# Value rounds of four batches of the 64-wide attention made while experts choose their tokens, and the first batch's first rounds at the expert stage's end

## The chip, the cores and the metric

One NeuronCore of a Trainium2 chip runs the whole kernel. The metric is the device time of one execution in microseconds (us); lower is better. PE is TensorE, DVE VectorE, ACT ScalarE, POOL GpSimd, SP the SyncE queue that issues most DMAs.

## The reference

Eight batches of 256 tokens, 256 wide, go through seven stages in float32. The change touches the second and the third: a mixture of experts where each expert chooses its tokens, and a cross-attention of 16 heads that are 64 wide.

```python
x = x + _L0_xattn_ref(_layernorm(x), ctx, ctx, ...)              # stage a0
x = x + _L0_ffn_ref(_layernorm(x), router_w1, router_w2, w1, w2, w3)   # stage f1
    probs = softmax((silu(h @ router_w1) @ router_w2).transpose(0, 2, 1))
    weights, tokens = top_k(probs, 64)               # 16 experts, 64 tokens each
    out = (silu(rows @ w1) * (rows @ w2)) @ w3       # then scatter-add by token
x = x + _L1_xattn_ref(_layernorm(x), ctx, ctx, Wq, bq, Wk, bk, Wv, bv, Wo)   # stage a2
    Q = h @ Wq.T + bq;  K = ctx @ Wk.T + bk;  V = ctx @ Wv.T    # 256 -> 1024
    out = softmax(Q K.T / 8) V, then @ Wo.T
```

K and V of stage a2 depend on the context and on weights alone, not on x.

## The kernel before

Every product is made of float32r halves: a value is split into a high part (ACT rounds it) and a low part (DVE subtracts), and each product is three passes. PE, DVE, ACT, POOL and SP each run their own program and meet by semaphores; a block barrier stands between stages.

**Stage f1** (`expert_choice_ffn`). PE transposes the normalised rows, makes the router's hidden layer and the logits. DVE then chooses 64 of 256 by eight rounds of max, max_index and match_replace (`choose`), PE turns the result over (`transpose_slots`), POOL gathers the first experts' rows from DRAM, and PE transposes them (`transpose_rows`). While `choose` and the gathers run PE has no work. Then come 16 experts: `up` and `down` on PE, about 18 us each, with gates on ACT, products on DVE and the scatter-add into x in DRAM (`scatter`) on POOL. SP writes the rows at the start (h_rows, x_rows), loads each next expert's weights, fetches the attention's weights (`prefetch`), and at the end reads x back as the scatters land. After its last scaling DVE makes the low parts of the attention's weights (`heads_low`), and the block ends.

**Stage a2** (`head_attention`). A batch has 16 steps s (head pair c = s // 2, half of the queries). In a step PE makes the scores of step s, transposes the probabilities of step s - 3, in every second step multiplies a pair's probabilities by the values (`weighted_values`, c = 0 to 7 at steps 5, 7, ... 15, and 1 and 3 of the next batch), and makes one projection round of the next batch. `output(b - 1)` stands at step 5; it waits for the low part of the pair c = 7, which DVE makes in step 4. The rounds are placed by a hand-written table; numbers from 16 on are steps of the batch's own run:

```python
STEP = {"hT": 6, ("k", 0): 7, ("q", 0): 8, ("k", 1): 10, ("q", 1): 11, ("v", 0): 12, ("k", 2): 13, ("v", 1): 14, ("q", 2): 15,
        ("k", 3): NU + 1, ("q", 3): NU + 2, ("v", 2): NU + LAG, ("v", 3): NU + LAG + 1}
```

A k or q round is 12 matmuls of 256 columns. ACT and DVE read it one step later into `k_fresh` or `q_fresh`, and SP copies it by six (k) or four (q) DMAs of 128 KB into the layout of the scores (`place`); ACT waits for that copy before it overwrites the buffer with the next k or q round. A v round is 6 matmuls of 512 columns, and DVE copies it into `vb`. The first batch has no earlier one to hide its rounds in: it makes `early` (k0, hT, v0, q0, v1, k1) before its first scores, and the others by `FIRST_STEP` in its steps 0 to 4. Batches 1 to 6 are a hardware loop on PE, DVE and ACT.

## Time and profile before

| | us |
|---|---|
| median of 3 runs | 1634.62 (1627.76 to 1641.94) |
| the profiled execution | 1631.33 |
| its span, first to last instruction | 1629.5 |
| PE busy | 1404.8 (86%) |
| DVE busy | 1078.6 (66%) |
| ACT busy | 841.1 (52%) |
| POOL busy | 480.4 (29%) |

Times within the trace are counted from the span's start. Stage f1 lasts from about 231 us to 576 us, stage a2 from there to about 997 us; a batch in the middle of a2 takes 49.0 us. A row of the timeline has start, duration, engine, line, operation with output<-input, and in brackets the idle time before it and what ended it. Durations of neighbours on one engine overlap, since operations are pipelined: the pitch is start to start.

### The profile page before, as it was taken

To read this page: it belongs to the slowest core of one execution; us is meant where nothing else is said; L and a number is where in the kernel's file an instruction comes from. 1 tells how busy PE (TensorE), PEld (TensorE's weight loads), DVE (VectorE), ACT (ScalarE), POOL (GpSimd) and SP (SyncE) were. 2 spreads that over 40 slices of the span, in tenths; PEclk is the share of its full clock that TensorE was granted. 3 is DMA by queue.
4 is the path that set the end of the run, shared out by engine and by line. 5 is a ranking of instruction groups with operands and counts; after the bars stand their busy time and mean duration, and the time that the engine had idled before them with its cause. 6 is when DMAs were issued, how large, how long until landed. Compare 5 with 4: busy or idle time off the path is not lost. (4 is left out here: it accounts for less than half of the span.)

```text
span 1629.5 us, 29259 instructions
## 1 busy us (share of the span) xinstructions
PE 1404.8 (86%) x9650; PEld 1133.9 (70%) x9650; DVE 1078.6 (66%) x2481; ACT 841.1 (52%) x1960; POOL 480.4 (29%) x426
## 2 busy tenths in 40 slices
PE   4899883999999959999999996599957799888885
PEld 4666552888888747888888884499945688655553
DVE  4577654666666557777877777644457774588776
ACT  2466652444444436666766676155534453565451
POOL 2111002577777530000000001255422521133343
PEclk7699996999999969999999999599978999899897
DMA  4322134456555456545544454022264010221110
GB/s 145 122 84 89 61 104 168 125 151 154 139 132 142 77 140 147 120 115 129 137 115 115 99 161 138 23 78 76 69 210 136 21 40 19 85 80 63 64 48 26
DMA packets 140110, 168.92 MB, mean 104 GB/s; under 512 B 20136, under 2 KB 131880, under 8 KB 137448
## 3 DMA queue, kind: packets, MB, share of 16 engines
q1 hardware_dynamic: 115032, 131.43, 27.9%
...
q14 instruction: 44, 0.36, 0.1%
...
## 5 line engine op out<-in xcount | busy, mean ns | idle before, releaser
L1046 DVE TENSOR_REDUCE a_nmax<-a_s 128x2 f32<-128x512 f32 x256 | 170.6, 684 | 99.6 <-PE a_s L961 99.1
L1245 ACT ACTIVATE a_probT<-a_t 128x512 f32<-128x512 f32 x256 | 151.8, 601 | 158.3 <-PE a_t L965 129.3
L63 POOL TENSOR_TENSOR a_rstd<-a_veps,minus_half 128x2 f32<-128x2 f32 x24 | 17.2, 715 | 413.8 <-DVE a_veps L57 413.7
L597 ACT ACTIVATE a_prob<-a_score,a_nmax 128x256 f32<-128x256 f32 x256 | 120.0, 479 | 35.0 <-DVE a_nmax L490 34.7
L490 DVE TENSOR_REDUCE a_nmax<-a_score 128x2 f32<-128x512 f32 x128 | 87.7, 685 | 73.5 <-PE a_score L383 73.4
L1782 POOL DMA_INDIRECT x_rows<-early_hn,scatter_row x60 | 129.5, 2158 | 16.4 <-issue 16.4
L1726 ACT ACTIVATE f_gate<-f_gate 128x512 f32<-128x512 f32 x64 | 38.3, 599 | 128.9 <-PE f_gate L1531 110.6
L1641 DVE TENSOR_TENSOR f_y<-f_gate,f_value 128x512 f32<-128x512 f32 x64 | 44.0, 687 | 82.0 <-PE f_value L1531 82.0
L606 ACT COPY a_probT<-a_T 128x512 f32<-128x512 f32 x128 | 76.1, 595 | 22.2 <-PE a_T L391 21.1
L497 DVE TENSOR_SCALAR a_prob<-a_prob,a_rinv 128x256 f32<-128x256 f32 x256 | 83.1, 367 | 4.6
L1542 PE MATMUL f_z<-area_odd_parts,f_y_hi 128*128 128x256 f32 x384 | 84.8, 287 | 0.4
L391 PE MATMUL a_T<-ident,a_prob 128*128 128x128 f32 x512 | 77.0, 273 | 4.2 <-DVE a_prob L497 4.2
L961 PE MATMUL a_s<-area_odd_parts 48*128 48x256 f32 x256 | 59.1, 330 | 24.8 <-DVE a_nmax L1046 14.9
L961 PE MATMUL a_s<-a_ka,a_qa 48*128 48x256 f32 x256 | 62.1, 348 | 17.9 <-DMA a_qa<-a_m_lo 6.2
L961 PEld LDWEIGHTS a_s<-area_odd_parts 48*128 48x128 f32 x256 | 37.0, 192 | 54.7 <-issue 29.1
L1531 PE MATMUL f_gate<-f_rowsT_hi,area_odd_parts 128*128 128x512 f32 x192 | 71.7, 400 | 1.5 <-DVE f_rowsT_lo L1629 1.5
L961 PEld LDWEIGHTS a_s<-a_ka,a_qa 48*128 48x128 f32 x256 | 40.0, 207 | 47.0 <-issue 30.9
L981 PE MATMUL a_o<-a_probT,a_vb 128*32 128x256 f32 x1024 | 71.7, 399 | 1.1 <-ACT a_probT L1245 1.1
L382 PE MATMUL a_score<-a_k_hi,a_q 128*128 128x256 f32 x256 | 70.3, 297 | 2.7 <-DMA a_q<-a_q_fresh_lo 2.0
L1531 PE MATMUL f_value<-f_rowsT_hi,area_odd_parts 128*128 128x512 f32 x192 | 71.3, 399 | 0.0
L402 PE MATMUL a_o<-a_probT,a_vb 128*64 128x256 f32 x512 | 69.4, 392 | 1.2 <-ACT a_probT L606 1.2
...
## 6 DMA issues: line engine op xcount, KB each, us to landing
...
a_k_hi<-a_k_fresh_hi SPq DMA_DIRECT2D x128, 128.0 KB, 2.4
...
a_k_lo<-a_k_fresh_lo SPq DMA_DIRECT2D x64, 128.0 KB, 2.4
a_q<-a_q_fresh_lo SPq DMA_DIRECT2D x64, 128.0 KB, 2.4
a_q<-a_q_fresh_hi SPq DMA_DIRECT2D x62, 128.0 KB, 2.4
a_ctxT<-in_ctxT SPq DMA_DIRECT2D x48, 128.0 KB, 2.7
...
```

Source lines behind the costliest of these rows:

```text
L391: last = nc.tensor.transpose(ps_T[u % 2][:, kc, i, :], prob[:, u % NPROB, i, kc * P:(kc + 1) * P], chip.ident[:, :])
L490: nc.vector.tensor_reduce(nmax[:, u % NPROB, :], ps_score[u % NB][:, :, :], AX.X, ALU.max, negate=True).then_inc(sem["nmax"], 1)
L497: last = nc.vector.tensor_scalar(prob[:, u % NPROB, i, :], prob[:, u % NPROB, i, :], rinv[:, u % NPROB, i:i + 1], None, ALU.mult)
L597: last = nc.scalar.activation(prob[:, u % NPROB, i, :], ps_score[u % NB][:, i, :], ACT.Exp, bias=nmax[:, u % NPROB, i:i + 1], accum_out=rs ...
L606: nc.scalar.copy(probT[:, c % 2, :, :, qt * P:(qt + 1) * P], ps_T[u % 2][:, :, :, :]).then_inc(sem["probT"], 1)
L961: last_s = nc.tensor.matmul(ps_s[i][:, half, :], qa[rows, u % RING, j, half * P:(half + 1) * P], ka[rows, u % RING, j, :], start=True, sto ...
L981: last = nc.tensor.matmul(ps_o[r * STRIP:(r + 1) * STRIP, :], vb[:, f % NV, kc, 4 * g + r, :], probT[:, (PPG * n + r // 2) % NPT, r % 2, k ...
L1046: nc.vector.tensor_reduce(nmax[:, u % 2, :, i * PPU + j], ps_s[i][:, :, :], AX.X, ALU.max, negate=True).then_inc(sem["nmax"], 1)
L1245: nc.scalar.activation(probT[:, t % NPT, i, :, :], ps_t[i][:, :, :], ACT.Exp).then_inc(sem["exp"], 1)
L1531: last = nc.tensor.matmul(ps[f % 2][:, :], W[:, kc, f * P:(f + 1) * P], h[:, kc, :], start=(kc == 0 and i == 0), stop=(kc == KC - 1 and i ...
L1542: last = nc.tensor.matmul(ps_z[s // 2][:, s % 2, :], h[:, f, s * P:(s + 1) * P], W[:, f, :], start=(f == 0 and i == 0), stop=(f == NF - 1 ...
L1782: nc.gpsimd.indirect_dma_start(chip.x_rows, bass.IndirectOffsetOnAxis(ap=scatter_row[:, q, s:s + 1], axis=0), chip.z_last[:, s, :] if last ...
```

## The change

A new `wide_front` holds what both stages share: the context of a batch, six PSUM banks, semaphores, and a DRAM tensor for values.

In stage f1, SP first loads four contexts (batches 1 to 4, eight DMAs of 128 KB) and the weights Wv are loaded a stage earlier. POOL rounds Wv and the contexts, DVE subtracts. After the logits PE makes 16 value rounds (4 batches x 4): ten ahead of `transpose_slots`, six behind it. ACT copies each into one of eight SBUF slots, SP writes each (256 KB) to DRAM. The low parts of Wk, Wq move from the end of the stage into the last expert's products, in pieces of 1024 columns; the first batch's context is loaded and split there, and after the last `down` PE makes k0, v0, v1, k1, v2, v3 of batch 0.

In stage a2, batch 0 begins with hT and q0; ACT instead of DVE copies its four v rounds; q3 moves from step 3 to step 4. Batches 1 to 4 have no v rounds: SP fetches each half of `vb` by one DMA of 512 KB, the first at step 12 of the batch before, ahead of the placing of q1, the second at step 4. Batches 5 to 7 are as before. The loops over batches are written out.

On PE, in stage f1, the order before had nothing between the last logits and the two turning operations (f_z<-f_routerT is the logits, f_slots the chosen tokens, early_hn the first gathered rows):

```order
L1496 MATMUL f_gate<-f_hT,area_odd 128x512 x2
L1504 MATMUL f_z<-f_routerT,area_odd 128x256 x4
L1511 MATMUL f_T<-ident,f_slots 128x128 x2
L1520 MATMUL f_T<-ident,early_hn 128x128 x8
L1531 MATMUL f_gate<-f_rowsT_hi,area_odd_parts 128x512
```

Now the last value round of sixteen, and the five before it of which one is shown, stand between the slots and the gathered rows (f_y_hi and f_y_lo hold the contexts here):

```order
L1654 MATMUL a2f_bank<-f_Wv_hi,f_y_hi 128x512 x2
L1654 MATMUL a2f_bank<-area_even_parts,f_y_hi 128x512 x2
L1654 MATMUL a2f_bank<-f_Wv_hi,f_y_lo 128x512 x2
L1654 MATMUL f_z<-f_Wv_hi,f_y_hi 128x512 x2
L1654 MATMUL f_z<-area_even_parts,f_y_hi 128x512 x2
L1654 MATMUL f_z<-f_Wv_hi,f_y_lo 128x512 x2
L1589 MATMUL a2f_bank<-ident,early_hn 128x128 x8
```

Ten more such rounds stand ahead of the slots. On PE, in steps 3 to 5 of a batch of a2, before (a_o is `weighted_values` of c = 7, 128x512 are v2 and v3; the product with a_oT_hi, the output, follows):

```order
L402 MATMUL a_o<-a_probT,a_vb 64x256 x4
L334 REGISTER_ALU
L362 MATMUL a_proj<-area_odd_parts,a_ctx_hi 128x512 x2
L362 MATMUL a_proj<-area_even_parts,a_ctx_hi 128x512 x2
L362 MATMUL a_proj<-area_odd_parts,a_ctx_lo 128x512 x2
L38 REGISTER_ALU
L382 MATMUL a_score<-a_k_hi,a_q 128x256
L383 MATMUL a_score<-a_k_lo,a_q 128x256
L382 MATMUL a_score<-a_k_hi,a_q 128x256
L383 MATMUL a_score<-a_k_lo,a_q 128x256
L391 MATMUL a_T<-ident,a_prob 128x128 x4
```

and in a batch without v rounds now:

```order
L447 MATMUL a2f_bank<-a_probT,a_vb 64x256 x4
L421 MATMUL a2f_bank<-a_k_hi,a_q 128x256
L422 MATMUL a2f_bank<-a_k_lo,a_q 128x256
L421 MATMUL a2f_bank<-a_k_hi,a_q 128x256
L422 MATMUL a2f_bank<-a_k_lo,a_q 128x256
L430 MATMUL a2f_bank<-ident,a_prob 128x128 x4
L421 MATMUL a2f_bank<-a_k_hi,a_q 128x256
L422 MATMUL a2f_bank<-a_k_lo,a_q 128x256
L421 MATMUL a2f_bank<-a_k_hi,a_q 128x256
L422 MATMUL a2f_bank<-a_k_lo,a_q 128x256
L430 MATMUL a2f_bank<-ident,a_prob 128x128 x4
L462 MATMUL a_proj<-area_odd_parts,a_oT_hi 128x256
```

The steps 3 and 4 have only scores, transposes and the one product with the values ahead of the output. On SP, at step 12, the fetch of values now stands between the placing of k1 and of q1:

```order
L329 DMA a_k_hi<-a_k_fresh_hi 64x2x256 x2
L329 DMA a_k_lo<-a_k_fresh_lo 64x2x256
L336 DMA a_vb<-a2f_values 128x2x512
L329 DMA a_q<-a_q_fresh_hi 64x2x256
L329 DMA a_q<-a_q_fresh_lo 64x2x256
```

Before, the copies of q1 followed those of k1 directly. The diff, cut to its core:

```diff
+    p.v_slots = 8
...
+    p.staged = range(1, 5)
+    p.v_dram = nc.dram_tensor(f"{stage}_values", (len(p.staged) * P, TB * 4 * D), F32).ap()
+    p.rounds = [("k", 0), ("v", 0), ("v", 1), ("k", 1), ("v", 2), ("v", 3)]
...
-    early = [("k", 0), "hT", ("v", 0), ("q", 0), ("v", 1), ("k", 1)]
-    FIRST_STEP = {("q", 1): 0, ("k", 2): 1, ("q", 2): 2, ("k", 3): 3, ("q", 3): 3, ("v", 2): 4, ("v", 3): 4}
+    early = ["hT", ("q", 0)]
+    FIRST_STEP = {("q", 1): 0, ("k", 2): 1, ("q", 2): 2, ("k", 3): 3, ("q", 3): 4}
...
+    VALUES_STEP = LAG + NCH + 1
...
+    without_v = [name for name in rounds if name[0] != "v"]
+    SPLIT_V = [f for f in range(B) if f not in p.staged]
...
+    def order(f):
+
+        return first_rounds if f == 0 else without_v if f in p.staged else rounds
...
         else:
-            own = [name for name in rounds if STEP[name] + delay == NU + s]
-        return [(name, b) for name in own] + [(name, b + 1) for name in rounds if more and STEP[name] + delay == s]
+            own = [name for name in order(b) if STEP[name] + delay == NU + s]
+        return [(name, b) for name in own] + [(name, b + 1) for name in (order(b + 1) if more else ()) if STEP[name] + delay == s]
...
+            if first(f) and name in ahead:
+                return ahead[name]
...
-            context(0)
...
+            def fetch_values(f, half):
+
+                sp.wait_ge(sem["pv"], (f - 1) * NCH + (half + 1) * NCH // 2)
+                values = p.v_dram[p.staged.index(f) * P:(p.staged.index(f) + 1) * P, :].rearrange("p (j e) -> p j e", j=TB)
+                at = slice(half * BANK, (half + 1) * BANK)
+                sp.dma_start(vb[:, :, at], values[:, :, at]).then_inc(sem["v_back"], 16)
+
             def places(b, more, part=None):
                 for s in range(NU):
+                    if s == VALUES_STEP and b + 1 in p.staged:
+                        fetch_values(b + 1, 0)
+                    if s == LAG + 1 and b in p.staged:
+                        fetch_values(b, 1)
...
+            for i in range(p.v_slots):
+                sp.wait_ge(p.sem[f"v_stored{i}"], 16 * (NV * len(p.staged) // p.v_slots))
...
                 if c % (NCH // 2) == 0:
-                    pe.wait_ge(sem["vb"], b * NV + (1 if c == 0 else 2) * TB)
+                    halves = 1 if c == 0 else 2
+                    if b in p.staged:
+                        pe.wait_ge(sem["v_back"], 16 * (2 * p.staged.index(b) + halves))
+                    else:
+                        pe.wait_ge(sem["vb"], SPLIT_V.index(b) * NV + halves * TB)
+                if first(b) and c == 1:
+                    pe.wait_ge(*consumed(0, ("k", 1)))
...
-            with pe.Fori(1, B - 1) as b:
-                batch(b, True)
-            batch(B - 1, False)
+            pe.wait_ge(sem["vb"], NV)
+            pe.wait_ge(*consumed(0, ("k", 0)))
+            for b in range(B):
+                batch(b, b + 1 < B)
...
-            context_low(0)
+            read_round(0, ("k", 0))
...
+            read_round(0, ("k", 0))
             zeros(0)
-            for name in early:
-                read_round(0, name)
-                if name == "hT":
-                    zeros(1)
-                if name == ("q", 0):
-                    place_first_queries()
-            batch(0, True)
-            with act.Fori(1, B - 1) as b:
-                batch(b, True)
-            batch(B - 1, False)
+            keep_first_v(0)
+            read_round(0, "hT")
+            for i in range(1, NV):
+                keep_first_v(i)
+            read_round(0, ("q", 0))
+            place_first_queries()
+            zeros(1)
+            read_round(0, ("k", 1))
+            for b in range(B):
+                batch(b, b + 1 < B)
...
+        V_SLOTS, V_BANKS, V_BEFORE = p.v_slots, 4, 10
+        values = [(f, half, t) for f in p.staged for half in range(2) for t in range(TB)]
+        staging = hT[:, :, :].rearrange("p k t -> p (k t)")
+        ps_T, ps_gate, ps_value = p.banks[0:2], p.banks[2:4], p.banks[4:6]
...
+            for n, f in enumerate(p.staged):
+                for kc in range(KC):
+                    sp.dma_start(raw_context[n][:, kc, :], chip.ctxT_dram[kc * P:(kc + 1) * P, f * S:(f + 1) * S]).then_inc(sem["v_context"], 16)
...
+            for n, (f, half, t) in enumerate(values):
+                sp.wait_ge(sem["v_kept"], n + 1)
+                rows_of_batch = slice(p.staged.index(f) * P, (p.staged.index(f) + 1) * P)
+                at = t * 4 * D + half * BANK
+                slot = n % V_SLOTS
+                sp.dma_start(p.v_dram[rows_of_batch, at:at + BANK], staging[:, slot * BANK:(slot + 1) * BANK]).then_inc(p.sem[f"v_stored{slot}"], 16)
...
+            for kc in range(KC):
+                sp.dma_start(p.ctxT[:, kc, :], chip.ctxT_dram[kc * P:(kc + 1) * P, 0:S]).then_inc(p.sem["ctx"], 16)
...
+            def value_round(n):
+
+                f, half, t = values[n]
+                h = p.staged.index(f)
+                if n == 0:
+                    pe.wait_ge(sem["v_lo"], KC)
+                pe.wait_ge(sem["v_context_lo"], h + 1)
+                if n >= V_BANKS:
+                    pe.wait_ge(sem["v_kept"], n - V_BANKS + 1)
+                _, _, Wv_lo = heads["v"]
+                hi, lo = context_hi[h], context_lo[h]
+                passes = [(c, W, kc) for c, W in ((hi, Wv_hi), (hi, Wv_lo), (lo, Wv_hi)) for kc in range(KC)]
+                for i, (c, W, kc) in enumerate(passes):
+                    last = nc.tensor.matmul(v_banks[n % V_BANKS][:, :], c[:, kc, t * P:(t + 1) * P], W[:, kc, half * BANK:(half + 1) * BANK],
+                                            start=(i == 0), stop=(i == len(passes) - 1))
+                last.then_inc(sem["v_ready"], 1)
+
+            for n in range(V_BEFORE):
+                value_round(n)
             transpose_slots()
+            for n in range(V_BEFORE, len(values)):
+                value_round(n)
             pe.wait_ge(sem["slot"], 4)
+            pe.wait_ge(sem["v_kept"], len(values))
             transpose_rows(0, 0, 0)
             pair_of(0, True)
...
+            def round_ahead(name, ps):
+
+                what, i = name
+                W, W_hi, W_lo = heads[what]
+                if what == "k":
+                    pe.wait_ge(sem["heads_lo"], KC)
+                else:
+                    W_hi = Wv_hi
+                if what == "v":
+                    half, j = divmod(i, TB)
+                    passes = [(c, W, kc) for c, W in ((p.ctx_hi, W_hi), (p.ctx_hi, W_lo), (p.ctx_lo, W_hi)) for kc in range(KC)]
+                    for n, (c, W, kc) in enumerate(passes):
+                        last = nc.tensor.matmul(ps[:, :], c[:, kc, j * P:(j + 1) * P], W[:, kc, half * BANK:(half + 1) * BANK],
+                                                start=(n == 0), stop=(n == len(passes) - 1))
+                else:
+                    passes = [(W, c, kc) for W, c in ((W_hi, p.ctx_hi), (W_hi, p.ctx_lo), (W_lo, p.ctx_hi)) for kc in range(KC)]
+                    for o in range(2):
+                        c0 = (2 * i + o) * P
+                        for n, (W, c, kc) in enumerate(passes):
...
+            pe.wait_ge(p.sem["ctx_lo"], 1)
+            for name, ps in zip(p.rounds, ahead):
+                round_ahead(name, ps)
...
+                        if last_expert:
+                            heads_low(f - 1)
...
+                    if last_expert:
+                        context_low()
+                        heads_low(3)
+                    weigh(e, q, last_expert)
...
-                    heads_low()
-                    dve.wait_ge(sem["heads_lo"], 1)
+                    nc.vector.tensor_scalar(heads["bq"], heads["bq"], heads["scale"], None, ALU.mult).then_inc(sem["heads_lo"], 1)
+                    dve.wait_ge(sem["heads_lo"], 2 * KC + 1)
...
+            _, _, Wv_lo = heads["v"]
+            for kc in range(KC):
+                dve.wait_ge(sem["v_hi"], kc + 1)
+                nc.vector.tensor_tensor(Wv_lo[:, kc, :], heads["v"][0][:, kc, :], Wv_hi[:, kc, :].bitcast(F32), ALU.subtract).then_inc(sem["v_lo"], 1)
+            low_weights(0, 0, 0)
+            for n in range(len(p.staged)):
+                dve.wait_ge(sem["v_context_hi"], n + 1)
+                nc.vector.tensor_tensor(context_lo[n], raw_context[n], context_hi[n].bitcast(F32), ALU.subtract).then_inc(sem["v_context_lo"], 1)
+            for n in range(1, 3):
...
-                        heads_high()
+                        context_high()
+                        heads_high(4)
+                        heads_high(5)
...
+            for n in range(len(values)):
+                act.wait_ge(sem["v_ready"], n + 1)
+                slot = n % V_SLOTS
+                if n >= V_SLOTS:
+                    act.wait_ge(p.sem[f"v_stored{slot}"], 16 * (n // V_SLOTS))
+                nc.scalar.copy(staging[:, slot * BANK:(slot + 1) * BANK], v_banks[n % V_BANKS][:, :]).then_inc(sem["v_kept"], 1)
...
+            for kc in range(KC):
+                nc.gpsimd.tensor_copy(Wv_hi[:, kc, :], heads["v"][0][:, kc, :]).then_inc(sem["v_hi"], 1)
             for g in range(E_G, GROUPS):
                 norm_rstd(nc, pool, chip, sem, nb, GT, g - E_G, g * GT)
+            pool.wait_ge(sem["v_context"], 16 * KC * len(p.staged))
+            pool.wait_ge(sem["hn"], GROUPS - E_G)
+            for n in range(len(p.staged)):
+                nc.gpsimd.tensor_copy(context_hi[n], raw_context[n]).then_inc(sem["v_context_hi"], 1)
...
+    w.values = (w.WvT, rows("WvT"))
...
-        dmas = [(w.WqT, rows("WqT")), (w.WkT, rows("WkT")), (w.WvT, rows("WvT")), (w.bq, a[prefix + "bq"]), (w.bk, a[prefix + "bk"])]
+        dmas = [(w.WqT, rows("WqT")), (w.WkT, rows("WkT")), *([w.values] if narrow else []), (w.bq, a[prefix + "bq"]), (w.bk, a[prefix + "bk"])]
```

## Rows read from the trace of the kernel before

**Rows 1.** Windows: length, busy time of PE, PEld, DVE, ACT, POOL, PEclk, DMA share, GB/s.

```profile
246.00:274.00 28.00, 2.89 (x12) 1.97 (x11) 15.41 (x56) 2.97 (x6) 8.34 (x11) 0.59 0.64 233
676.00:725.00 49.00, 47.87 (x368) 40.80 (x364) 36.92 (x103) 34.03 (x108) 0.69 (x1) 1.00 0.52 124
```

**Rows 2.** Timeline of PE, from the end of the experts to the first scores.

```profile
567.02 0.28 PE L1542 MATMUL f_z<-f_W_hi,f_y_lo 128*128 128x256 f32 x1
582.52 0.80 PE L370 MATMUL a_proj<-a_ctx_hi,area_odd_parts 128*128 128x256 f32 x2 [15.22 <-DVE a_ctx_lo L456]
...
592.14 0.40 PE L370 MATMUL a_proj<-a_hT_hi,area_even_parts 128*128 128x256 f32 x2
...
598.04 0.36 PE L382 MATMUL a_score<-a_k_hi,a_q 128*128 128x256 f32 x1 [1.97 <-DMA a_q<-a_q_fresh_lo]
```

**Rows 3.** Timeline of SP at the start of a2: x comes back.

```profile
577.51 3.29 SPq L291 DMA_DIRECT2D x_tok<-x_rows  x2
```

**Rows 4.** Timeline of DVE, the first norm of stage a2.

```profile
576.62 0.75 DVE L49 BATCH_NORM_STATS2 a_stats<-x_tok 128x6 f32<-128x256 f32 x2 [1.73 <-PEq L1405]
...
582.38 0.73 DVE L70 TENSOR_SCALAR a_hn<-x_tok,a_mv,a_rstd 128x256 f32<-128x256 f32 x2
```

**Rows 5.** Timelines of PE and of ACT, steps 4 to 7 of batch 0.

```profile
617.24 0.73 PE L362 MATMUL a_proj<-area_odd_parts,a_ctx_hi 128*128 128x512 f32 x2 [2.11 <-DVE a_k_fresh_lo L469]
...
618.07 0.84 ACT L585 ACTIVATE a_q_fresh_hi<-a_proj,area_even 128x256 fp32r<-128x256 f32 x2 [1.79 <-DMA a_q<-a_q_fresh_lo]
...
622.37 1.08 PE L402 MATMUL a_o<-a_probT,a_vb 128*64 128x256 f32 x8
...
627.59 0.50 PE L370 MATMUL a_proj<-a_ctx_hi,area_odd_parts 128*128 128x256 f32 x2 [0.67 <-DVE a_ctx_lo L456]
```

**Rows 6.** Timeline of PE in f1, the choice and the first expert.

```profile
260.78 0.69 PE L1511 MATMUL f_T<-ident,f_slots 128*128 128x128 f32 x2 [14.59 <-DVE f_slots L1609]
270.49 1.94 PE L1520 MATMUL f_T<-ident,early_hn 128*128 128x128 f32 x8 [9.02 <-DMA early_hn<-h_rows,f_gather_row]
273.92 0.76 PE L1531 MATMUL f_gate<-f_rowsT_hi,area_odd_parts 128*128 128x512 f32 x1 [1.49 <-DVE f_rowsT_lo L1629]
```

**Rows 7.** Timeline of PE in a middle batch, steps 13, 3, 4 and 5.

```profile
691.97 1.08 PE L402 MATMUL a_o<-a_probT,a_vb 128*64 128x256 f32 x8
...
709.18 0.72 PE L362 MATMUL a_proj<-area_odd_parts,a_ctx_hi 128*128 128x512 f32 x2
...
710.68 0.28 PE L382 MATMUL a_score<-a_k_hi,a_q 128*128 128x256 f32 x1
...
714.88 0.36 PE L417 MATMUL a_proj<-area_odd_parts,a_oT_hi 128*128 128x256 f32 x1 [0.66 <-DVE a_oT_lo L502]
```

**Rows 8.** Timeline of ACT in that batch, step 12.

```profile
690.37 0.84 ACT L585 ACTIVATE a_q_fresh_hi<-a_proj,area_even 128x256 fp32r<-128x256 f32 x2 [1.50 <-DMA a_q<-a_q_fresh_lo]
691.10 0.59 ACT L606 COPY a_probT<-a_T 128x512 f32<-128x512 f32 x1
```

**Rows 9.** Timeline of DVE in that batch, steps 2 to 4.

```profile
707.59 0.88 DVE L469 SCALAR_TENSOR_TENSOR a_k_fresh_lo<-a_proj,area_even,a_k_fresh_hi 128x256 fp32r<-128x256 f32 x2 [0.86 <-ACT a_k_fresh_hi L585]
...
712.84 0.68 DVE L477 COPY a_vb<-a_proj 128x512 f32<-128x512 f32 x1
...
714.16 0.47 DVE L502 SCALAR_TENSOR_TENSOR a_oT_lo<-a_o,area_even,a_oT_hi 128x256 fp32r<-128x256 f32 x1
```

**Rows 10.** Timeline of SP in that batch: the first copy of q1.

```profile
692.44 0.61 SPq L303 DMA_DIRECT2D a_q<-a_q_fresh_hi  x1
```

**Rows 11.** DMA issues, 630 to 770 us: count, size, median us to landing.

```profile
a_q<-a_q_fresh_lo SPq DMA_DIRECT2D x24, 128.0 KB, 2.4
area_odd<-in_L_W SPq DMA_DIRECT2D x3, 512.0 KB, 4.1
```

**Rows 12.** Timelines of POOL and of DVE in batch 0: two that overlap.

```profile
603.33 4.56 POOL L670 TENSOR_TENSOR area_even_parts<-area_even,area_odd_parts 128x2048 fp32r<-128x2048 f32 x1
...
603.50 4.80 DVE L497 TENSOR_SCALAR a_prob<-a_prob,a_rinv 128x256 f32<-128x256 f32 x2
```

155 lines of the change are left out of this document (94 added, 61 removed).

## The prediction

> **What bounds the kernel now.** I read the windows view first, to see stages and not the whole span. Between 246 and 274 us, while f1 chooses tokens, PE is busy 2.89 of 28 us and its granted clock is 0.59, near the lower of its two levels (1.2 and 2.4 GHz) [rows 1]. In a middle batch of a2 PE is busy 47.87 of 49.00 us at clock 1.00, DVE 36.92, ACT 34.03 [rows 1]: PE bounds that stage on average. The timelines then show what each engine waits for at single places. Between stages PE is empty for 15.22 us (567.3 to 582.5), then works with gaps until the first scores at 598.04 [rows 2]. So there are two holes (28 and 31 us) and a stage full of PE work; the change takes 16 value rounds from the stage and puts them into the first hole, and six rounds of batch 0 into the second. What that is worth has to be read where the rounds stood, not from the average.
>
> **Part 1: the choice in f1.** Ten value rounds run from the last logits to the slots. The product over the slots starts at 260.78 after 14.59 us of idleness, so PE is free from 246.19 [rows 6]. A value round is 6 x 512 columns; in a2 such a round and its successor start 710.68 - 709.18 = 1.50 us apart, a hand-over of about 0.1 included, at clock 1.00 [rows 7]. Ten take 14.0 to 15.0 us and end at 260.2 to 261.2, so the slots are turned 0 to 0.4 us late. The six behind take 8.4 to 9.0 us more and end near 270.3; ACT's copy of the last adds 0.6 (its copy of the same shape, 0.59, [rows 8]). The gathered rows are ready at 270.49 [rows 6]: 0.4 us late, at most 1. PE is then warm for the first expert: before, eight transposes took 1.94 us and the first products ran on the slow clock (0.76 for the first) [rows 6]. I take +0.7 for lateness and -1.7 for the clock: **-1 us**, bounds -2.5 and +2.
>
> First what the rows show on another risk of this part: a POOL tensor_tensor that started at 603.33 took 4.56 us, and a DVE scaling that started at 603.50 and is short elsewhere took 4.80 [rows 12]. The Trainium skill, "SBUF — State Buffer", who interferes with whom, has it that a DVE instruction with two SBUF inputs and a POOL one that reads SBUF block each other in full; the trace agrees in that DVE stood for the whole of POOL's instruction. By that rule POOL's six new roundings would hold up DVE's six new subtractions ahead of `choose`, and the sum would be about 1.5 us less good.
>
> **Part 2: between the stages.** The block ends when SP has issued the reading back of x's first half, which waits for the scatters; DVE starts a2 at 576.62 after a wait of 1.73 us for the barrier [rows 4]. The change does not touch the scatters. The six rounds ahead take 4 x 1.5 (v) + 2 x 1.5 (k) = 9.0 us at most, from 567.3 to 576.3: just inside. The low parts that moved into the last expert cost nothing, since they stand where each other expert's weights are split; without that cover they would be two more DVE instructions on the way to the last product, about 1.2 us each.
>
> In a2 the norm ends at 583.1 now (start 582.38), because it stands behind the subtraction of the context, which waits for a DMA issued at the stage's start [rows 4]. Afterwards it stands behind the reading of k0, which is in PSUM at once: statistics to 577.9, k0 low to 578.7, norm to 579.4. Transposes 1.0, high and low part 1.3, q0 2.6 (cold), so q0 ends near 584.3, with 0.1 per hand-over; from q0's end to the scores it is 598.04 - 592.54 = 5.5 us now [rows 2], which gives 589.8. The SP queue says a little later: x comes back until 580.8 [rows 3], the next context and six copies of k0 take 5.9, two of q0 1.5 and 2.4 to land [rows 11]: 590.6. **-7.4 us**; bounds -8.5 (q0 warm) and -5.
>
> **Part 3: batch 0.** v2 and v3 are gone from step 4 and q3 stands there. Before, v2 waited 2.11 us and pair 0's product came at 622.37 [rows 5]. Now that product waits only for ACT's copy behind k3's high part; k3's low part, 0.9 us behind the high one, ended at 617.2 [rows 5], so the high part at about 616.3 and the copy at 616.9. ACT reads q3 at 618.07, when q2's copies have landed [rows 5]; behind that stand three steps of about 1.5 us (copy 0.5, exponentials 1.0) and the context's two parts, 1.2, so k0 of batch 1, at 627.59 before [rows 5], comes at about 623.2 to 624. **-4.4 us**; bounds -6 (two rounds and the 2.11 wait given back) and -2.
>
> **Part 4: batches 1 to 4.** Sixteen rounds of 1.48 us leave PE: 23.7 us, if all of it comes back. I do not think so. Each batch's four rounds stand in steps 12, 14, 3 and 4, followed by the output, which starts at 714.88 and waited for DVE's low part of c = 7 [rows 7]. Step 12: ACT reads q1 only at 690.37, since q0's copies had not landed, and its next copy ends at 691.7; the product with the values at 691.97 needs that copy [rows 7, 8]. So of v0 only 0.3 us comes back. Of v1 (step 14) about 1.2: the product of step 15 waits for ACT's copy behind k2's high part. PE's q2 then ends 1.5 us earlier, DVE's k3 low (707.59) about 1.4. From there DVE runs without a pause to the low part at 714.16; only one of the two v copies, 0.60 us, stands ahead of that [rows 9]. So the output starts 2.05 us earlier, not 5.9, and in place of the rest PE idles ahead of it. DVE's chain is late next. After the output all engines are in step as before. Four batches: **-8.2 us**.
>
> The fetches: 512 KB takes 4.1 us to land where 128 KB takes 2.4 [rows 11], so one holds the DMA engines about 1.7 us. The values are wanted some 20 us later, that is hidden. But the first fetch goes into SP ahead of q1's copies, which start at 692.44 in an unbroken row [rows 10]: they come 0.65 (issue) to 2.4 us later, and land about 698.1, just ahead of ACT's reading of q2. I cost it at nothing; without that cover, 1.5 us each time.
>
> **Sum.** -1 - 7.4 - 4.4 - 8.2 = -21.0 against 1631.33 of the profiled execution: 1610.3. That execution is 3.3 us under the median of the three; I give 1611 (the sum on the median would be 1613.6).
>
> **The rivals.**
> - *PE gets everything back.* For it: PE is 98% busy in a batch and DVE is not full. Against: the waits above. Part 4 becomes -23.7: 1594.8.
> - *Nothing comes back in the batches*, because q1's late copies hold ACT at q2: part 4 is 0 to -3: 1618.5 down to 1615.5. For it: SP's copies follow each other unbroken and ACT already waits 1.50 us for one [rows 8].
> - *The choice overflows.* If the value rounds run on the lower clock (twice 1.4, 2.8 us a round), sixteen take 45 us from 246.2 and the first rows are transposed at 291.7 rather than 270.5: +21.2 in place of -1, 1632.5. For it: the clock is lower as soon as PE waits in that hole. Against: the rounds follow the logits without a pause, and four banks and eight slots lie between PE, ACT and the stores. The Trainium skill, "TensorE: Matmul & The Clock Gate", the HAM clock gate, has it that PE is throttled by default and sustained work releases it, so the clock would hold here.
> - *Slower than before: the fetches end up in the placing chain.* Place: SP's queue at steps 12 and 4 of batches 0 to 4. If each of the eight delays the next copies by its whole 4.1 us and ACT, hence PE, stands for it, part 4 becomes +32.8: 1651. It decides from 12.8 / 8 = 1.6 us a fetch on. Against: at step 4 only q3's copies are near, which are wanted eight steps later.
>
> **How the numbers follow.** Forecast 0.53, everything back 0.13, nothing back 0.15, overflow 0.11, slower 0.08. The range 1595 to 1623 holds the first three; the other 19 in 100 lie above. What a measurement of this kernel can tell from no change is about 1%, that is under 1618.3 for faster. Faster: 0.53 + 0.13 + 0.10 of the third = 0.76; within 1%: 0.05 + 0.11 + 0.01 = 0.17; slower 0.07. The forecast's own range is 1603 to 1618: all bounds of the parts at once would be wider, but they are independent.
>
> **What would show it.** Right: PE nearly full from 246 to 270 at clock 1.00 and the first rows at about 270.9; first scores 13 to 14 us after a2's start (21.4 now); batches with fetched values of 47 us, with about 2.7 us of idleness ahead of each output, put down to DVE's oT_lo; batches 5 to 7 at 49. Wrong: a staged batch of 43 to 44 us (then my waits were not firm), or of 49 and more with ACT waiting for a_q or a_k copies (then the fetches collide); the slots turned after 262 (then the overflow).

## The result, and the profile after

| | before | changed kernel |
|---|---|---|
| median of 20 runs each, us | 1637.3 | 1626.99 (1615.46 to 1638.29) |
| ratio, 95% interval | | 0.9941 (0.9921 to 0.9961) |
| the profiled execution, us | 1631.33 | 1626.16 |

The changed kernel is about 10 us faster, 0.6%: within 1% of before. The prediction said 1611 us, 21 less than its profile of before, and a range up to 1623. Half of the gain did not come. The forecast starts from the one profiled execution of before, 1631.33 us, which lies 6 us under the median of the twenty runs.

The windows view of the changed kernel (columns as in [rows 1]), four batches of a2 from output to output; the first three have fetched values:

```profile
658.90:706.40 47.50, 42.55 (x340) 36.30 (x340) 34.47 (x100) 33.66 (x107) 0.69 (x1) 1.00 0.61 150
706.40:753.60 47.20, 43.31 (x340) 36.90 (x340) 34.49 (x100) 33.75 (x107) 0.69 (x1) 0.98 0.63 151
753.60:802.70 49.10, 43.57 (x341) 37.11 (x341) 34.60 (x100) 33.73 (x107) 0.69 (x1) 0.98 0.62 146
802.70:853.00 50.30, 49.40 (x364) 42.37 (x364) 36.17 (x103) 34.36 (x107) 0.69 (x1) 0.97 0.56 133
```

PE has 4.3 to 5.3 us less to do in a staged batch (one with fetched values: 42.6 to 43.6 busy, 47.87 in [rows 1]), yet only the first two of the three are shorter than 49.0 us, by 1.5 and 1.8 us. Only in the first row is the clock at 1.00 throughout.

The timeline of PE in f1, which answers to [rows 6]:

```profile
264.36 0.44 PE L1580 MATMUL a2f_bank<-ident,f_slots 128*128 128x128 f32 x2 [0.81 <-DVE f_slots L1727]
275.79 1.07 PE L1589 MATMUL a2f_bank<-ident,early_hn 128*128 128x128 f32 x8 [2.69 <-DMA early_hn<-h_rows,f_gather_row]
278.52 0.77 PE L1600 MATMUL a2f_bank<-f_rowsT_hi,area_odd_parts 128*128 128x512 f32 x1 [1.66 <-DVE f_rowsT_lo L1747]
```

The slots come 3.6 us later than before, all of it lost before f1; the rows come 5.3 us later, though PE and ACT had finished the sixteen rounds and waited 2.69 us for a gather. DVE's start of a2 and PE's first scores, which answer to [rows 4] and [rows 2]:

```profile
581.92 0.75 DVE L49 BATCH_NORM_STATS2 a_stats<-x_tok 128x6 f32<-128x256 f32 x2 [7.91 <-PEq L1454]
```

```profile
595.73 0.55 PE L421 MATMUL a2f_bank<-a_k_hi,a_q 128*128 128x256 f32 x1 [5.49 <-DMA a_q<-a_q_fresh_lo]
```

The scores come 13.81 us after a2's start (21.42 before): what was forecast. Where PE waits in the first of those windows (timeline; of PE's idle times over 0.15 us between 658.9 and 706.5 only one of 0.47 at 669.77, which before has too, is not among them):

```profile
689.70 1.08 PE L447 MATMUL a2f_bank<-a_probT,a_vb 128*64 128x256 f32 x8 [1.59 <-ACT a_probT L649]
694.47 1.08 PE L447 MATMUL a2f_bank<-a_probT,a_vb 128*64 128x256 f32 x8 [0.24 <-ACT a_probT L649]
704.24 0.39 PE L421 MATMUL a2f_bank<-a_k_hi,a_q 128*128 128x256 f32 x1 [1.66 <-ACT a_prob L640]
706.42 0.39 PE L462 MATMUL a_proj<-area_odd_parts,a_oT_hi 128*128 128x256 f32 x1 [1.00 <-DVE a_oT_lo L547]
```

From both traces, stage by stage (starts of the instructions named; hT(n) are the transposes of batch n's rows):

| stretch | before | after | difference |
|---|---|---|---|
| start to f1 (first transposes of h) | 231.1 | 234.7 | +3.6 |
| f1 to the first expert's first product | 42.8 | 43.9 | +1.0 |
| to the last `down` | 293.1 | 294.2 | +1.1 |
| to the first scores | 31.0 | 23.0 | -8.0 |
| to hT(1) | 26.4 | 22.4 | -4.0 |
| hT(1) to hT(5), the staged batches' rounds | 196.3 | 194.0 | -2.4 |
| to the last output | 169.7 | 170.7 | +1.0 |
| to the end | 639.1 | 641.6 | +2.5 |

The last stretch holds nothing that the change touches, and the one ahead of it only the loops written out. In 19 traces of this study the last stretch took 632.3 to 650.9 us, in kernels of every kind, so one pair of traces says little of it; the same goes for f1's start.

### The profile page after: what moved, and what is told of

Read it like the earlier page. It is cut to its first block and busy times, and to the rows that moved or that the text cites. A ratio compares the mean times of both kernels' runs of the same rounds, so it can differ in the third digit from the quotient of the medians.

```text
span 1624.4 us, 28649 instructions
## 1 busy us (share of the span) xinstructions
PE 1408.3 (87%) x9650; PEld 1134.5 (70%) x9650; DVE 1071.5 (66%) x2468; ACT 850.3 (52%) x1983; POOL 484.0 (30%) x432
## 5 line engine op out<-in xcount | busy, mean ns | idle before, releaser
L1095 DVE TENSOR_REDUCE a_nmax<-a_s 128x2 f32<-128x512 f32 x256 | 170.7, 685 | 101.7 <-PE a_s L1010 101.4
L640 ACT ACTIVATE a_prob<-a2f_bank,a_nmax 128x256 f32<-128x256 f32 x256 | 120.2, 480 | 39.2 <-DVE a_nmax L535 39.1
L1600 PE MATMUL a2f_bank<-f_rowsT_hi,area_odd_parts 128*128 128x512 f32 x384 | 134.4, 401 | 1.7 <-DVE f_rowsT_lo L1747 1.7
L535 DVE TENSOR_REDUCE a_nmax<-a2f_bank 128x2 f32<-128x512 f32 x128 | 87.8, 686 | 67.0 <-PE a2f_bank L422 66.9
L1861 ACT ACTIVATE f_gate<-a2f_bank 128x512 f32<-128x512 f32 x64 | 38.3, 599 | 124.6 <-PE a2f_bank L1600 98.9
L1759 DVE TENSOR_TENSOR f_y<-f_gate,a2f_bank 128x512 f32<-128x512 f32 x64 | 44.0, 688 | 80.4 <-ACT f_gate L1861 36.7
L1600 PEld LDWEIGHTS a2f_bank<-f_rowsT_hi,area_odd_parts 128*128 128x128 f32 x384 | 73.2, 191 | 19.2 <-issue 1.9
L421 PE MATMUL a2f_bank<-a_k_hi,a_q 128*128 128x256 f32 x256 | 72.8, 306 | 12.9 <-ACT a_prob L640 7.3
L649 ACT COPY a_probT<-a2f_bank 128x512 f32<-128x512 f32 x128 | 76.2, 596 | 12.9 <-PE a2f_bank L430 11.6
L430 PE MATMUL a2f_bank<-ident,a_prob 128*128 128x128 f32 x512 | 78.1, 276 | 3.6 <-DVE a_prob L542 3.6
L447 PE MATMUL a2f_bank<-a_probT,a_vb 128*64 128x256 f32 x512 | 70.3, 396 | 10.0 <-ACT a_probT L649 9.1
```

What stands on the lines that cost most here:

```text
L430: last = nc.tensor.transpose(ps_T[u % 2][:, kc, i, :], prob[:, u % NPROB, i, kc * P:(kc + 1) * P], chip.ident[:, :])
L535: nc.vector.tensor_reduce(nmax[:, u % NPROB, :], ps_score[u % NB][:, :, :], AX.X, ALU.max, negate=True).then_inc(sem["nmax"], 1)
L640: last = nc.scalar.activation(prob[:, u % NPROB, i, :], ps_score[u % NB][:, i, :], ACT.Exp, bias=nmax[:, u % NPROB, i:i + 1], accum_out=rs ...
L649: nc.scalar.copy(probT[:, c % 2, :, :, qt * P:(qt + 1) * P], ps_T[u % 2][:, :, :, :]).then_inc(sem["probT"], 1)
L1095: nc.vector.tensor_reduce(nmax[:, u % 2, :, i * PPU + j], ps_s[i][:, :, :], AX.X, ALU.max, negate=True).then_inc(sem["nmax"], 1)
L1600: last = nc.tensor.matmul(ps[f % 2][:, :], W[:, kc, f * P:(f + 1) * P], h[:, kc, :], start=(kc == 0 and i == 0), stop=(kc == KC - 1 and i ...
```

## Experiments

Seventeen more runs followed, two of them of the changed kernel and of the kernel before as they are. Ratios are to the kernel before, timed on the same chip. Where nothing is said, an edit is made to the changed kernel.

**A second trace.** No edit.

> The changed kernel once more, nothing edited, for a second trace. In its first trace a0 ended 3.56 us later than before although nothing in it waited for the new load of Wv, and two of the four batches with fetched values held a fall of the granted clock for 3.4 us, at the holes ahead of the output (751.7 and 802.9). Theory A (clock by chance in a0, clock falls at the new holes in the batches): f1 starts between 229 and 235, on either side of 231.1; the transposes of the first rows come again 11.4 us after the slots, against 9.7 before; the first scores 13.8 us after a2's start; staged batches 47.2 to 47.5 us where the clock stays at its upper level, and again one to three falls in the staged batches or right behind them. Theory B (the new load delays a0): f1 starts at 234 to 235 again. Ratio to the kernel before 0.992 to 0.996 for both.

Ratio 0.9946 (0.9921 to 0.9970). f1 starts at 238.3, later than either theory had it, the rows come 11.07 after the slots, the four periods from hT(1) to hT(5) are 49.6, 47.7, 47.8, 47.9, and the clock does not fall between 625 and 960: this count missed.

**The rounds ahead alone.**

```diff
-    p.staged = range(1, 5)
+    p.staged = range(1, 1)
```

The value rounds in f1 and the waits for them are taken out with it.

> No batch is staged: no value rounds in f1, no stores, no fetches, all batches after the first make their own four value rounds; the six rounds ahead at the expert stage's end stay, and the new split of Wv at f1's start too. All outputs are computed. Theory A: what the changed kernel gains is parts 2 and 3 (7.6 and 4.0 us in its trace), and the staged batches give back what f1 loses: this kernel is 11 to 12 us faster than before (ratio 0.993), that is the same as the changed one within 2 us; rows of the first expert 9.7 us after the slots, no fall of the clock between 660 and 940, batches 49.0. Theory of the prediction (parts 1 and 4 worth 9.2 us): this kernel is 9 us slower than the changed one, ratio 0.999 if the changed one is at 0.994.

Ratio 0.9939 (0.9915 to 0.9963), the same as the changed kernel; rows 9.92 after the slots, four periods 197.2 us, no fall. All the gain is in parts 2 and 3; parts 1 and 4, forecast at 9.2 us, bring nothing that can be measured: the two ratios differ by 0.0002, and each is known to about 4 us.

**What delays the gathers in f1.** First, only the fetch of a2's weights is held:

```diff
+            sp.wait_ge(sem["rowsTp"], KC)
             prefetch(sp, sem["wload"])
```

> The changed kernel, but SP waits until the first expert's rows have been transposed before it issues the fetch of a2's weights (3 MB), which in the changed kernel goes out at 274.1, in the middle of the gathers. Theory A (the gathers share the DMA engines with that fetch, which the sixteen stores pushed from 244.9 to 274.1): the rows come 2.8 us after the fourth gather's start as before, not 4.8; the first up 1.5 to 2 us earlier against the slots; time 2 us (0.12%) less than the changed kernel. Rival (the value stores themselves fill the DMA engines, 256 KB each until 273.7): the rows still come 4.8 us after the fourth gather, and the time is that of the changed kernel.

The rival was right: the rows come 4.85 us behind the fourth gather (ratio 0.9961, 0.9936 to 0.9987). Then the last eight stores are held too:

```diff
                 sp.wait_ge(sem["v_kept"], n + 1)
+                if n == V_SLOTS:
+                    sp.wait_ge(gathered[0], GATHERS)
```

> The changed kernel, but SP holds the last eight stores of values (and the fetch of a2's weights behind them) until the first expert's rows have been gathered; the first eight are issued by 262 as before. Holding that fetch alone left the rows 4.85 us behind the fourth gather's start. Theory E (the stores, 256 KB every 1.4 us, share the DMA engines with the gathers): rows 2.8 to 3.0 us behind the fourth gather, 9.7 us behind the slots (11.4 in the changed kernel), then the transposes wait for the last value round instead and come at 9.7 to 10; time 1.5 us less than the changed kernel. Rival (PE's or ACT's value work delays the rows): they still come at 11 or more.

The fourth gather and the rows, in this kernel (timelines of POOL and PE):

```profile
278.22 0.95 POOL L1931 DMA_INDIRECT early_hn<-h_rows,f_gather_row  x1 [0.30 <-issue]
```

```profile
281.07 1.07 PE L1591 MATMUL a2f_bank<-ident,early_hn 128*128 128x128 f32 x8 [0.78 <-DMA early_hn<-h_rows,f_gather_row]
283.79 0.47 PE L1602 MATMUL a2f_bank<-f_rowsT_hi,area_odd_parts 128*128 128x512 f32 x1 [1.65 <-DVE f_rowsT_lo L1749]
```

2.85 us, against 4.77 in the changed kernel and 2.81 before; the first product comes 41.9 us after f1's start (43.9; 42.8 before), and the last `down` 293.06 later (294.22). Ratio 0.9916 (0.9886 to 0.9945). It was the stores, since with the fetch of a2's weights held in both kernels only they differ: with them out of the way part 1 is worth 0.9 us, as forecast.

**The load of Wv in a0.** In the changed kernel ACT issues it at 54.61 (`area_even<-in_L_WvT`), behind the first expert's weights. PE then, in the timeline:

```profile
64.84 0.55 PE L1010 MATMUL a_s<-a_ka,a_qa 48*128 48x256 f32 x1 [5.42 <-DMA a_qa<-a_m_lo]
```

and a0's copies of q just issued, in the DMA view from 59.4 to 66 of the changed kernel, and from 63.2 to 69 of before (KB each, median us to landing):

```profile
a_qa<-a_q_hi SPq DMA_DIRECT2D x4, 64.0 KB, 3.6
```

```profile
a_qa<-a_q_hi SPq DMA_DIRECT2D x4, 64.0 KB, 2.6
```

The kernel before again, then with this load alone (`[*dmas, *also]` in the fetch of a0, as in the change):

> The kernel before once more, for a second trace of it. In the five traces of kernels that load Wv during a0, f1 starts at 233.5 to 241.6 (mean 237.1); in the one trace of before at 231.1, though its clock was low for 41 us at the start against 27. Theory C (the load of Wv, issued at 54.6, delays a0 by about 4.4 us: queries issued at 59.5 land after 4.3 us instead of 2.5 and PE stands idle): f1 starts at 229 to 234. Theory D (a0's length is chance of the clock alone): f1 starts anywhere from 231 to 241, as in the others.

> The kernel before with one part of the change: the 1 MB of Wv is loaded in a0 (behind the first expert's weights) and no longer in f1. Theory C: 4 to 6 us slower than before (ratio 1.0025 to 1.0035), f1 starts at 235 to 240, the three stages behind as before. Theory D: same time as before (ratio 0.999 to 1.001).

f1 starts at 232.7 without and at 233.6 with the load (235 to 240 was expected), but the stretch of a0 that holds it (from the 17th to the 33rd of DVE's maxima) takes 26.0 and 31.7 us. Ratio of the second 1.0022 (0.9997 to 1.0046): in the forecast's direction, not beyond its interval. Then the load taken out of a0, as f1's first DMA:

```diff
+            sp.dma_start(*heads["values"]).then_inc(sem["v_raw"], 16)
             for n, f in enumerate(p.staged):
```

> The changed kernel with Wv loaded by SP as the first DMA of f1 instead of in a0; POOL makes its norm's powers first and rounds Wv behind them. Theory C: f1 starts at 229 to 234, the slots are turned 29.7 us later as before, and the time is 4 to 6 us less than the changed kernel's, ratio to before 0.990 to 0.992. Theory D: f1's start is as scattered as in the changed kernel and the ratio stays 0.994 to 0.995. If the load delays f1 instead, the slots come later than 29.7 us after f1's start.

Ratio 0.9934 (0.9907 to 0.9961). The stretch is 26.0, but the slots come 31.5 us after f1's start instead of 29.7: DVE waits for the rounded Wv ahead of `choose`. And at a0's end, once the last scores are made, first without staging, then in the changed kernel:

```diff
+            if behind:
+                sp.wait_ge(sem["st"], 2 * PPU * NUNIT)
+            for dst, from_dram in behind:
+                sp.dma_start(dst, from_dram).then_inc(sem["wload"], 16)
```

> The kernel without staged batches (only the six rounds ahead remain of the change), with Wv loaded by SP at the end of a0 behind the last scores. Theory C (that load at 54.6 costs a0 4 us): ratio 0.991 to 0.992, f1 starts at 229 to 236, and from there 42.8 us to the first expert's first product, first scores 13.8 us behind a2's start. Theory D (its place is free): 0.994 as without the edit.

> The changed kernel with the load of Wv alone moved to the end of a0 (stores, fetches and a2 as in the changed kernel). In fourteen traces so far the stretch of a0 from the 17th to the 33rd of DVE's maxima took 26.5 us (25.3 to 27.5) in the five without the load at 54.6, and 30.7 us (27.6 to 33.7) in the nine with it. Theory C: 4 us less than the changed kernel, ratio 0.991 to 0.992, that stretch 25 to 27.5. Rival (the later stretches of a0 give it back, as the ratio 0.994 of the kernel without staging and with this edit says): ratio 0.994 to 0.995 with that stretch as short.

0.9940 (0.9917 to 0.9963) in the first, no gain; 0.9918 (0.9890 to 0.9947) in the second, 4 us. Over all 19 traces the stretch takes 26.7 us (24.8 to 28.6) in the ten without the load at 54.6 and 30.7 (27.5 to 33.8) in the nine with it; f1 starts at 232.8 and at 237.5 on average. In all nine with the load PE once stands idle there for 4.5 to 7.0 us, in the other ten for at most 3.1. So the load costs about 4 us where it lands, in the mean of these traces. The timed pairs say 4, 4 and 0, each with 4 to 5 us of uncertainty: the delay is shown, its size at the end is not settled. The two traces of the changed kernel itself show the stretch at 27.6 and 27.5 us, no longer than the 27.5 of before, but at granted clocks of 0.88 and 0.81 against 0.72; the 3.6 us by which f1 starts later in the first table arise behind it (156.4 us from the 33rd maximum to f1, 152.4 before), where the clock was lower (0.96 against 0.98). How the clock and the load share these 3.6 us stays open.

**The batches: fetches.** `fetch_values` returns at once, and PE does not wait for it.

> The changed kernel without the eight fetches of values and without the wait for them: batches 1 to 4 weigh what stands in the buffer (the values of batch 0), so the output of a2 is not the reference's; everything else runs. Theory A (the fetches are hidden, the batches keep their holes because ACT waits for the copies of k and q and DVE's chain is late ahead of the output): staged batches stay at 47.2 to 47.5, time within 1.5 us of the changed kernel. Rival (fetches collide with the copies of k and q, so ACT waits longer): batches at 45.5 to 46.5, the hole of 1.6 us at step 12 halves, time 4 to 6 us (0.3%) less.

Ratio 0.9927 (0.9890 to 0.9963), from nine of twelve executions; the median of all twelve, 1629.57 us, is 0.996 of before's, so the time does not show that the fetches cost anything. The traces do. The four periods are 48.0, 46.9, 48.0 and 47.4, 190.3 us in all although the clock fell once; the second trace of the changed kernel, without any fall, has 192.9. That is 0.65 us a batch, or more if the fall is counted.

What a fetch holds up are the copies of q1 that are issued behind it. In the DMA view, first of the changed kernel from 731.9 to 737 us, then of this one from 736 to 741, both at step 12 of the same batch:

```profile
a_q<-a_q_fresh_hi SPq DMA_DIRECT2D x2, 128.0 KB, 4.7
```

```profile
a_q<-a_q_fresh_hi SPq DMA_DIRECT2D x2, 128.0 KB, 2.4
```

ACT must see them landed before it reads q2, and PE stands behind ACT (the changed kernel, timelines of ACT and PE):

```profile
740.34 0.84 ACT L628 ACTIVATE a_q_fresh_hi<-a_proj,area_even 128x256 fp32r<-128x256 f32 x2 [0.98 <-DMA a_q<-a_q_fresh_lo]
```

```profile
741.71 1.08 PE L447 MATMUL a2f_bank<-a_probT,a_vb 128*64 128x256 f32 x8 [1.33 <-ACT a_probT L649]
```

Without fetches this hole is 0.24 us in the same batch. In the seven traces with a fetch at step 12 the four copies of q1 behind it take 4.6 us (median of 112), and ACT waits for them at q2 in 22 of 28 batches, for 0.7 to 2.0 us; in the twelve other traces, with no fetch at this place, it never does (counting waits over 0.15 us). The Trainium skill, "DMA: Bandwidth & Descriptors", issuing engines are not separate DMA queues, has it that transfers issued by SP, ACT and POOL interleave on the same 16 engines; the traces agree in a0 (a load issued on ACT, felt by SP's copies) and in f1 (stores issued by SP, felt by POOL's gathers).

The hole of 1.59 us at 689.70 is another one. Here ACT waits at k2 for the last copy of k1, which was issued 0.67 us **ahead** of the fetch (timelines of SP and ACT):

```profile
684.29 0.62 SPq L329 DMA_DIRECT2D a_k_lo<-a_k_fresh_lo  x1
684.96 0.60 SPq L336 DMA_DIRECT2D a_vb<-a2f_values  x1
685.61 1.53 SPq L329 DMA_DIRECT2D a_q<-a_q_fresh_hi  x1
```

```profile
688.33 0.84 ACT L628 ACTIVATE a_k_fresh_hi<-a_proj,area_even 128x256 fp32r<-128x256 f32 x2 [1.40 <-DMA a_k_lo<-a_k_fresh_lo]
```

From the DMA view, 684.9 to 690 us:

```profile
q8 instruction: 1, 0.02, 1.3%
a_k_lo<-a_k_fresh_lo SPq DMA_DIRECT2D x1, 128.0 KB, 4.0
```

That copy takes 4.0 us instead of 2.4, but not because of the fetch: in 18 batches a fetch was issued at step 12 behind k1's last copy and no packet of an instruction queue ran while the copy was under way, and it landed after 2.4 us. Over these four batches of all 19 traces, 19 such copies had an instruction packet of about 1 us beside them and took 3.1 to 4.8 us, nine of them in kernels without a fetch at this step, this one included; the 57 without took 2.41 to 2.46. So the late k1 goes with fetches of instructions, in one to three of the first batches of nearly every kernel with staging, and removing the fetches of values leaves it (holes of 1.51 and 0.89 us).

The fetch moved behind the copies of k2, and 0.64 us of DVE's work out of the chain ahead of the output:

```diff
-    VALUES_STEP = LAG + NCH + 1
+    VALUES_STEP = NU - 1
...
-                    if more and s == 2:
+                    if more and s == LAG + 1:
                         norm_apply
```

> The changed kernel with the two edits in a2 alone: the fetch at step 15 and the normalised rows at step 4. Theory (a fetch ahead of q1's copies makes ACT, hence PE, late at step 12, as its hole fell from 1.2 to 1.6 us to 0.3 to 0.9 without fetches; and DVE's 0.64 us stand in its chain ahead of the output): the hole at step 12 is under 1 us, those of 1.66 and 1.0 together 2.0 instead of 2.66, staged batches 46.3 to 46.9 where the clock holds, 3 to 5 us less than the changed kernel. Rival (one hole goes and the next opens, since ACT's and DVE's chains are as long as the step): batches stay at 47.2 to 47.9, ratio 0.994.

Ratio 0.9911 (0.9880 to 0.9942), the 5 us expected, though this is no more than the two intervals allow by chance; periods 47.7, 48.1, 47.1, 48.8, longer than expected, with three falls of the clock, and 48.2 in batches 5 and 6, which have no hole. ACT's wait for q1's copies is gone. The hole that goes with a late k1 stays, 1.85 and 1.78 us in the first two batches where under 1 was expected, and in the last two ACT waits 0.44 and 1.55 us for copies of q2, which the fetch at step 15 now has ahead of it.

**The batches: the clock.** What a fall looks like in the changed kernel (windows ahead of the output at 802.67, and behind it):

```profile
799.50:802.90 3.40, 1.41 (x10) 1.18 (x11) 3.33 (x11) 3.15 (x11) 0.00 (x0) 1.00 0.88 202
802.90:806.30 3.40, 3.40 (x17) 3.40 (x17) 0.99 (x4) 1.15 (x5) 0.00 (x0) 0.50 0.84 195
806.30:809.70 3.40, 3.40 (x30) 3.40 (x30) 0.00 (x0) 0.00 (x0) 0.00 (x0) 1.00 0.71 234
```

PE, with its two holes, was busy for 1.41 of 3.40 us; then it was busy without a pause, at 0.50 (1.2 GHz), and made 17 products where the same time at full clock saw 30. Fillers in the holes:

```diff
+                    if s == LAG + 1 and b in p.staged:
+                        filler(b, 7)
                     scores(b, s)
...
+                if b + 1 in p.staged:
+                    filler(b + 1, 4)
                 pe.wait_ge(sem["oT_lo"], (b + 1) * NCH)
```

> The changed kernel with products that nobody reads put into the two holes of each staged batch: seven of 512 columns ahead of the scores of step 4, where PE stood idle for 1.66 us, four ahead of the output, where it stood idle for 1.0 us. Seen so far: in six traces with staged batches the clock fell for 3.4 us or more nine times between 615 and 970, in four traces without them never. Theory F (the holes bring the falls): no fall between 615 and 970, the staged batches all at 47.5 to 48.0, time 1 to 3 us less than the changed kernel (ratio 0.992 to 0.994). Rival (the falls have another cause, such as the fetches or the code written out): falls as before, batches of 49 to 50 among them, ratio 0.994 to 0.995.

No fall in the staged batches; 47.6 and 47.3 in the middle, 49.1 and 48.9 at the ends, where 47.5 to 48.0 was expected for all. The ratio, 0.9946 (0.9923 to 0.9968), shows no gain. Between 625 and 960 us, nine traces with staged batches and no fillers have 19 falls in 36 such batches, 18 of them within 2 us of the start of an output that stands behind a staged batch's steps 3 and 4, the other right behind a hole of 1.78 us at step 12. Eight traces without staging, 32 batches at the same place, have none; two with fillers, 8 batches, none. So the holes bring the falls. The Trainium skill, "TensorE: Matmul & The Clock Gate", the HAM clock gate, has it that the clock depends on how busy PE has lately been; the traces agree in that the falls come behind holes and nowhere else in these batches.

**All together.** The held stores, the load at a0's end and the two edits in a2, all shown above:

> The changed kernel with four edits: Wv is loaded by SP at the end of a0 behind the last scores (the DMA engines are empty there from 193 on) instead of at 54.6; the last eight stores are held until the first rows are gathered; the first fetch of a batch's values is issued at step 15 behind the copies of q1 and k2, not at step 12 ahead of those of q1; DVE makes the next batch's normalised rows at step 4 behind the low part that the output waits for, not at step 2. If the causes found so far are right (load of Wv 4 us, stores against gathers 2 us, fetches 0.8 us a batch, DVE's chain ahead of the output 0.6 us a batch): 10 to 11 us less than the changed kernel, ratio to before 0.987 to 0.989. f1 starts at 229 to 236, rows 9.6 us behind the slots, staged batches 46.3 to 46.9 where the clock holds. If the load's place and the fetches do not matter: 0.992 as with the held stores alone.

Ratio 0.9845 (0.9801 to 0.9890), from six executions: 25 us less than before, 1% less than the changed kernel, more than expected. f1 starts at 231.5, the rows 9.50 after the slots, the periods are 47.5, 48.1, 47.2, 47.8 with three falls. With four and three fillers in the holes that remain:

> The kernel with all four edits (ratio 0.9845), and in the holes of its staged batches four products of 512 columns that nobody reads ahead of the scores of step 4, three ahead of the output. In its trace the clock fell three times, for 3.4 us each, at these holes. Theory F: no falls between 600 and 960, staged batches 46.3 to 47, 2 to 4 us less, ratio 0.982 to 0.983. Rival (the fillers themselves are in the way): batches 47 to 48, ratio 0.985 or more.

The trace does nearly what theory F says: no fall between 625 and 960 (one at 606, in batch 0, where every kernel here has one), and 47.2, 46.4, 46.9, 46.7. The windows of the middle two:

```profile
655.20:701.60 46.40, 44.25 (x347) 37.57 (x347) 34.49 (x100) 33.70 (x107) 0.69 (x1) 1.00 0.63 152
701.60:748.50 46.90, 44.25 (x347) 37.62 (x347) 34.65 (x100) 33.70 (x107) 0.69 (x1) 1.00 0.65 154
```

The time does not show it: 0.9848 (0.9812 to 0.9884), again from six. 3.4 us are less than these intervals resolve. What of the 25 us needs the staged batches, and what would help any kernel (`p.staged = range(1, 1)` with the load at a0's end and `norm_apply` at step 4; then `norm_apply` at step 4 in the kernel before):

> No staged batches, but the two edits that need none: Wv loaded at the end of a0, and the next batch's normalised rows made at step 4 instead of 2. Against the kernel with all four edits (ratio 0.9845), this tells what the staged batches are worth once stores, fetches and the load no longer collide. Theory G (from the traces: f1 1.2 us shorter, four batches 190.6 us instead of 193.4): 4 us slower than that kernel, ratio 0.987. Rival (staging gives nothing even then, its holes and the clock falls in them take it back): the same ratio, 0.984 to 0.986, with batches of 48.2.

> The kernel before with one edit that the change does not have: the next batch's normalised rows at step 4 instead of 2 (and PE waits for the low part of Wo in the loop as well, which has long been there). Theory G: batches 5 to 7 of the kernels with this edit took 48.2 instead of 48.8, so here six batches gain 0.6 each: 3 to 4 us, ratio 0.9975, no holes. Rival (the edit helps only where PE has holes): 1.000 and batches of 49.0.

0.9897 (0.9860 to 0.9935) without staging, and 0.9976 (0.9951 to 1.0002) for the one edit on the kernel before, with batches of 48.3. So staging, worth nothing as built, seems to be worth something once its transfers are out of the way: 8 us by the timed ratios (0.9845 and 0.9848 against 0.9897, with an uncertainty as large), 4 to 8 by the traces (190.5 and 187.1 us for the four batches against 193.5 and 193.7, and 1.2 in f1).

**The loops written out.**

> The kernel before with its loops over batches written out on PE, DVE, ACT and POOL, and nothing else. In the traces between 612 and 960 us the instruction queues move 13 packets before and 36 in the changed kernel, and issues of SP's copies of k and q that take over 1.0 us instead of 0.6 number 3 before and 11 after, landings over 2.9 us 10 and 56 (26 without staged batches). Theory H (written-out code costs fetches of instructions, which hold SP's issues and the copies beside them): 9 to 12 slow issues, 20 to 30 slow landings; the batches of 49.0 hide them, so the time stays within 2 us of before (ratio 0.999 to 1.001). Rival (the slow landings come from the change's own transfers): 3 slow issues and 10 slow landings as before. A third case: the code written out costs the batches time, 0.3 us each or more, ratio 1.001 to 1.003, which would be part of what the change lost.

Theory H: 36 packets of instructions, 11 slow issues and 25 slow landings, ratio 0.9982 (0.9955 to 1.0010), batches 48.8. In the kernel before, written-out loops cost nothing. In the staged kernels their instruction packets meet k1's copies, as shown above, and there ACT waits at k2 for up to 2.2 us (0.4 at most in the eight traces without staging). A staged kernel that keeps its loops was not run, so what this costs is not known.

## Why the prediction was wrong

- **The load of Wv (not in the sum).** The prediction took every cost from the places that the change speaks of; the load that it moved into a0 was mentioned ahead of it and priced nowhere. In the mean of the traces it costs about 4 us where it lands, since PE waits there for small copies. In the timed pairs it is 4, 4 and 0.
- **Part 1, -1 us; measured +1.0, and +1.1 in the first expert.** The rounds did what was forecast: slots 29.70 us after f1's start (29.68 before), transposes of the rows 1.07 us instead of 1.94. The step that failed is "the gathered rows are ready at 270.49": it took the gathers' time from a trace that has no such stores. Sixteen stores of 256 KB made it 1.7 us longer; PE then waited 2.69 and 1.66 us, and the clock fell again for 6.8 us in the first expert, which took back the warm start. With the stores held the term is -0.9. The overflow did not happen. Nor did POOL's roundings delay the slots, and the 1.5 us given for them did not come: one pair of them took 3.39 us beside DVE's subtractions and the next 2.08, but `choose` was done in time. The row that this risk was read from [rows 12] has a scaling of DVE beside POOL, not a subtraction of two tensors.
- **Part 2, -7.4; measured -8.0.** Right, path and size: 13.8 us from a2's start to the scores (13 to 14 forecast), a wait for q's low copies at the end. The low parts moved into the last expert did cost nothing.
- **Part 3, -4.4; measured -4.0.** Right.
- **Part 4, -8.2; measured -2.4, and -0.3 in the mean of the six traces with the same a2 (192.9 to 197.9 us, against 196.2 in six without staging).** The idleness ahead of the output has the size that was forecast, 1.66 + 1.00 = 2.66 us (2.7), though only the 1.00 waits for DVE's low part and the 1.66 for ACT's probabilities; batches 5 to 7 take 48.8 (49). Three things beside it failed. "I cost it at nothing" of the fetch: it is about 0.7 us a batch, and by the way that was weighed and dismissed. The copies of q1 behind it do not land "just ahead of ACT's reading of q2"; they take 4.6 us, and ACT stands for them 0.7 to 2.0 us. The late copies of k1, which go with instruction fetches, were not thought of. And the holes themselves were counted only as time not gained: two falls a trace, each 3.4 us or more at half the clock, take another 1.7 us each of the following work. The clock was treated as a stage's property (1.00), and not as something that the change's own idle times could lower.
- **The rivals.** "Nothing comes back in the batches" (0.15) is what happened to part 4, and its cause, q1's late copies holding ACT at q2, is there in the traces; the falls of the clock and the late copies of k1 come on top. The range, up to 1623, assumed that at least parts 1 to 3 come whole and that no stage outside the diff's two is touched. Measured from the forecast's own starting point, 1631.33, the gain of about 10 us would give 1622, just inside it: 6 of the 16 us between forecast and time lie in the execution started from, the rest in the terms above.

The terms as now known: 4 (load, the uncertain one), 2 (f1), -8.0, -4.0, -0.3, in all about -6, against a measured -9.6 (-12.9 to -6.4). The part of a2 behind hT(5) and the later stages scatter by more than this difference; it stays open.
